# Layer two's row-major causal mask moves from TensorE to VectorE in a two-layer transformer kernel

## What is computed

```
xn = layernorm(x)
x  = x + attention0(xn) + ffn0(xn)              # layer one, 16 heads, gated ffn of width 704
xn = layernorm(x)
# layer two: latent attention, 16 heads of 16 features, latent width 64
c      = layernorm(xh @ Wdkv) * ln_g + ln_b
scores = (xh @ absorbed) @ c.T / sqrt(64)
scores = where(tril, scores, -inf)              # the causal mask
w      = softmax(scores)
x = x + (w @ (c @ Wuv)) @ Wo_h @ Wo.T + bo + experts(xn)   # 32 experts, top 6, and a shared one
```

## Time and profile before

| | us |
|---|---|
| median of three runs | 2020.04 (2015.65 to 2021.65) |
| the profiled execution | 2017.58, its span 2015.8 |
| TensorE busy | 1746.5 |
| VectorE busy | 1100.9 |
| GpSimd busy | 874.7 |
| ScalarE busy | 819.5 |
| VectorE, maxima of `q_rows` (L1224), 256 times | 130.6 |
| TensorE, mask products of `q_rows` (L1611), 256 times | 70.6 |

### The profile page before, as it was taken

The page is one execution under the profiler, slowest core; times in us unless marked ns, Lnnn a source line. Parts: engine busy times, 40 slices in busy tenths (PEclk is TensorE's granted clock), DMA queues, the critical chain, the costliest instruction groups (busy, mean ns, idle before and its releaser), DMA issues.

```text
span 2015.8 us, 41842 instructions
## 1 busy us (share of the span) xinstructions
PE 1746.5 (87%) x16112; PEld 1333.6 (66%) x16112; DVE 1100.9 (55%) x2557; ACT 819.5 (41%) x1596; POOL 874.7 (43%) x995
## 2 busy tenths in 40 slices
PE   3657898989999998989989898999989899888887
PEld 2434676767677676767767676776767677675766
DVE  5645373655647365664737465473746547364442
ACT  2532435344343534334353433435353443534332
POOL 2312343535354454435444353534535353543455
PEclk7878999999999999999999999999999999999999
DMA  5632222313142231314132141413213141321221
GB/s 129 163 85 62 59 59 64 81 43 87 37 102 53 74 73 51 76 40 105 47 83 64 51 87 36 107 37 91 56 53 85 37 107 37 93 54 46 54 64 33
DMA packets 323318, 139.26 MB, mean 69 GB/s; under 512 B 227568, under 2 KB 308528, under 8 KB 323120
## 3 DMA queue, kind: packets, MB, share of 16 engines
q1 hardware_dynamic: 304688, 86.23, 18.5%
q0 software_dynamic: 18432, 50.36, 9.1%
HBM read 102.12 MB, written 29.88 MB: 65 GB/s over the span
## 4 chain that ended last, share of the span: by engine, by line
PE 26%; issue 25%; DVE 19%; POOL 17%; ACT 8%; SPq 3%; DMA 2%; POOLq 0%; DVEq 0%; ACTq 0%
PE s3r L1394 7%; POOL gs L762 6%; POOL h2l L771 5%; POOL cb L741 3%; PE s2acc L1391 3%; DVE th L1269 3%; DVE mx L1102 3%; PE s1a L1394 2%; DVE gs L1274 2%; PE s2r L1394 2%; PE s1acc L1497 2%; POOL h1p L706 2%; PE s1a L1514 2%; ACT h2h L967 1%; ACT p L876 1%
## 5 line engine op out<-in xcount | busy, mean ns | idle before, releaser
L771 POOL TENSOR_TENSOR h2l<-th,h2h 128x512 f16<-128x512 f32 (+1 forms) x224 | 246.5, 1103 | 390.9 <-ACT h2h L967 380.5
L762 POOL TENSOR_TENSOR gs<-gs,cb 128x512 f32<-128x512 f32 x192 | 243.9, 1270 | 263.6 <-DVE gs L1274 262.2
L967 ACT CAST h2h<-th 128x512 f16<-128x512 f32 (+1 forms) x224 | 131.2, 586 | 425.8 <-DVE th L1269 356.9
L1394 PE MATMUL s3r<-xe,xg 128*128 128x256 f16 x2304 | 284.5, 273 | 2.7 <-DVE gs L1274 2.7
L1391 PE MATMUL s2acc<-xd,h2h 128*128 128x256 f16 x1536 | 263.9, 274 | 24.5 <-POOL h2l L771 24.5
L1394 PE MATMUL s3r<-xe,xu 128*128 128x256 f16 x2304 | 283.0, 273 | 1.6 <-DVE th L1269 1.6
L1394 PEld LDWEIGHTS s3r<-xe,xg 128*128 128x128 f16 x2304 | 222.7, 98 | 39.9 <-DVE gs L1274 8.7
L1394 PEld LDWEIGHTS s3r<-xe,xu 128*128 128x128 f16 x2304 | 223.7, 98 | 31.6 <-DVE th L1269 5.5
L741 POOL DMA_DIRECT2D cb<-comb_d x384 | 229.0, 604 | 20.9 <-issue 11.2
L1274 DVE SCALAR_TENSOR_TENSOR gs<-th,s3r 128x512 f32<-128x512 f32 (+1 forms) x224 | 143.9, 642 | 148.8 <-ACT th L971 148.4
L1269 DVE TENSOR_TENSOR th<-s3r,gs 128x512 f32<-128x512 f32 x192 | 132.1, 688 | 168.5 <-POOL gs L762 164.5
(11 more groups left out here) (280 smaller groups left out, 3140.4 us busy)
## 6 DMA issues: line engine op xcount, KB each, us to landing
cb<-comb_d POOLq DMA_DIRECT2D x128, 192.0 KB, 3.4
part_d<-part SPq DMA_DIRECT2D x32, 512.0 KB, 3.3
cb<-comb_d POOLq DMA_DIRECT2D x128, 128.0 KB, 3.0
stacks<-part_d SPq DMA_DIRECT2D x192, 64.0 KB, 2.4
va<-v_d SPq DMA_DIRECT2D x512, 8.0 KB
cb<-comb_d POOLq DMA_DIRECT2D x128, 64.0 KB, 3.0
land<-part_d SPq DMA_DIRECT2D x96, 64.0 KB, 2.7
part<-part_d SPq DMA_DIRECT2D x96, 64.0 KB, 3.5
```

Of the source, the lines that this page charges most:

```text
L762: g.tensor_tensor(gc2[:, p % 2, :], gs2[:, p % 2, :], cb2[:, 2 * (p % 6):2 * (p % 6) + 2, :].rearrange("p a s -> p (a s)"), ALU.mult).then ...
L771: g.tensor_tensor(h2l[0:m, n % 2, 0:w], th2[0:m, n % 2, 0:w], h2h[0:m, n % 2, 0:w], ALU.subtract).then_inc(sem("h2l_made"), 1)
L967: s.copy(h2h[0:m, n % 2, 0:w], th2[0:m, n % 2, 0:w]).then_inc(sem("h2h_made"), 1)
L1394: ins = nc.tensor.matmul(bk, lhs[i][k], rhs[j][k], start=first, stop=last)
```

## The change

The mask products of layer two's row-major scores leave TensorE. `maskq1` becomes 256 columns wide: 128 zeros, then the causal block. VectorE runs, for each head, two instructions that add the mask, write the sum back into the bank in place, and keep the row maximum: one over columns 0 to 127 with the causal block, one over columns 128 to 383 with all of `maskq1`. Each writes its maximum straight into `mx2`, so `m32` and the folding go, and TensorE's transposition waits for the last bank's release. The wait for the bank is put on an instruction of its own (`carry`). All 25 order strings are other ones of the same lengths and the same counts of digits; the body's strings of TensorE and VectorE are shown.

```diff
-        "body": ("022020012122001121002101022221120220212100142212101012131301200103100101031101310120001003"
-                 "34300300403040003043343303001333133"),
+        "body": ("022201021222010100101201202211220200112121021221121201301302001041001010331013110010030203"
+                 "14300300403040003403313030333403133"),
...
-        "body": ("020202011120012120010212122020212212012102021211120121130103001100001000303003010112100002"
-                 "44033040340330331030314303310333431"),
+        "body": ("020212021100210101200212212022120210021110212212121101023210300101001120000000031310130410"
+                 "43033304000004333130300331341330334"),
...
-        maskq1 = sb("maskq1", [P, P], BF16)
+        maskq1 = sb("maskq1", [P, S], BF16)
...
-                v.tensor_reduce(m32[:, h, :], bk[:, 0:3 * P].rearrange("p (c n) -> p c n", n=P), AX.X, ALU.max).then_inc(empties2(u), 1)
-                if n == H - 1:
-                    dve.wait_ge(*emptied2(it, u))
-                    v.tensor_copy(mx2[:, :, 0], m32[:, :, 0]).then_inc(sem("max2_folded"), 1)
-                    v.tensor_tensor(mx2[:, :, 1], m32[:, :, 1], m32[:, :, 2], ALU.max).then_inc(sem("max2_folded"), 1)
+                carry(dve, "dve_waited")
+                v.tensor_tensor_reduce(bk[:, 0:P], bk[:, 0:P], maskq1[:, P:S], 1.0, -3.0e38, ALU.add, ALU.max, mx2[:, h, 0:1])
+                v.tensor_tensor_reduce(bk[:, P:3 * P], bk[:, P:3 * P], maskq1[:, :], 1.0, -3.0e38,
+                                       ALU.add, ALU.max, mx2[:, h, 1:2]).then_inc(empties2(u), 1)
...
-            v.tensor_scalar(maskq1[:, :], mask_tmp[1], -BIG, None, ALU.add).then_inc(sem("dve_const"), 1)
+            v.memset(maskq1[:, 0:P], 0.0)
+            v.tensor_scalar(maskq1[:, P:S], mask_tmp[1], -BIG, None, ALU.add).then_inc(sem("dve_const"), 1)
...
-                    mm(bk[:, P * j:P * j + P * (j + 1)], query(qst2, h, OPEN)[:, P * j:P * j + P],
-                       key(kst2, h, OPEN)[:, 0:P * (j + 1)], start=j == 0, stop=False, skip_group_check=True)
-                mm(bk[:, 0:3 * P].rearrange("p (c n) -> p c n", n=P)[:, 0:3:2, :], identb[:, :],
-                   maskq1[:, :].unsqueeze(1).to_broadcast([P, T, P]), start=False, stop=True,
-                   skip_group_check=True).then_inc(fills2(u), 1)
+                    ins = mm(bk[:, P * j:P * j + P * (j + 1)], query(qst2, h, OPEN)[:, P * j:P * j + P],
+                             key(kst2, h, OPEN)[:, 0:P * (j + 1)], start=j == 0, stop=j == T - 1, skip_group_check=True)
+                ins.then_inc(fills2(u), 1)
                 if n % 2:
                     yield
-            pe.wait_ge(*event("max2_folded", it, 2))
+            pe.wait_ge(*emptied2(it, U2["q_rows", H - 1]))
```

More of the change, by code:

```diff
@@ L81 @@
     "sp": {
[L82 to L91, removed]
+        "body": ("020121001110000112201112102321311101112220301300230331002002203023200132020021031304330323"
+                 "03200021200144411034143001003003110"),
@@ new lines @@
+        "start": ("230011010310112020300201020300120003102211023004121013030231130041142312012020200133030013"
+                 "31020401313101214022013201302403210"),
+        "first": ("111001023131200001012010220313100330020001312011330313022202313102222123011412003100110341"
+                 "32002000040021042100034313100312402"),
+        "late": ("202201000201112022110012221201111110122210103132002332304021031042233243022100033300101303"
+                 "10034000303300141014000101013000331"),
@@ L92 @@
+        "end": ("402041221000010141001201112002213001210010020120013233333320321021233103002303123343011100"
+                 "01000001110113013202222030030101424"),
     },
     "pe": {
-        "body": ("022020012122001121002101022221120220212100142212101012131301200103100101031101310120001003"
-                 "34300300403040003043343303001333133"),
-        "start": ("200201120110120100000311100022002402000120001030001130103323023312204102130041332101330121"
-                 "01243103103221023312234302140103101"),
@@ new lines @@
+        "start": ("100100010000311010020100020000210020013003212210233004311031014111202000224102121230311242"
+                 "13033122300232232303131401301334110"),
+        "first": ("012004102011122133210013001302000303120101002211101203100101201201311101031211302301230024"
+                 "03312004010040000222420303333403322"),
+        "late": ("220201201222002141010221001220224411202021121212101103213102133001301400100130101300131031"
+                 "00030300003030300214000340313310333"),
@@ L104 @@
+        "end": ("200200040210120104221010212212041002000021224221211210020102010100031213103421031110030033"
+                 "01331310033001330101304033130331023"),
     },
     "dve": {
-        "body": ("020202011120012120010212122020212212012102021211120121130103001100001000303003010112100002"
-                 "44033040340330331030314303310333431"),
-        "start": ("000020200002021220310010000000211220110100301312001013030043213001330012214011124022331010"
-                 "11302132341111123200212032301334343"),
@@ new lines @@
+        "start": ("020122102110011200003011000200000000020212030324113033231142312332042312301003010101031011"
+                 "11130230020114010210203432413323201"),
+        "first": ("010011022211102303001121000200031200110212230211130300101010020000101300001311011140112233"
+                 "23410323214034220300020432433323320"),
+        "late": ("022102201421021201200100122024122210012212121112121220101311310300402130140001000100100333"
+                 "00030133000403300033010430131333330"),
@@ L116 @@
+        "end": ("221100012212100002012220112112222022112411142211210000230040102331102010031310310004010000"
+                 "40000033031310003433331033031331003"),
     },
     "act": {
[L118 to L127, removed]
+        "body": ("021222001110221201100022210101222000011201201000210212011223113101201010311310000033241043"
+                 "00020403043030043130300133331343303"),
@@ new lines @@
+        "start": ("111212000221101000021311200000020010011202120010010301230200333040332401301002110322232311"
+                 "11402103333413001040021211332300243"),
+        "first": ("211220112103001011103320120000200201000101123110201002100223113111310131120210123220403003"
+                 "24012300340200402320300403033303341"),
+        "late": ("024041022004022211200101121220222110411121022220121241310130000010031133321010101011300000"
+                 "10303003200014302303000301333333103"),
@@ L128 @@
+        "end": ("220021000102101021000221011220021204012102202020420120122310100311113113211344331101042300"
+                 "33021300334013000330001313033013000"),
     },
     "gp": {
[L130 to L139, removed]
+        "body": ("022001104222100100224022120221202020120021102002002000100300343111330000300012111100123011"
+                 "03413301113331400203313431033011331"),
@@ new lines @@
+        "start": ("123011000131101414231014220200102403303013301100000043233023220100022021131132201432100110"
+                 "01110223202031001220332013110003000"),
+        "first": ("202220200031042030201110124102103020100100304212201010120033031331002201243303313020240100"
+                 "10133001023412300033012110123111101"),
+        "late": ("202412422200042201200112022102101012022212012111200001033010011110040301300201031303030031"
+                 "14003331113310231302031300330040301"),
@@ L140 @@
+        "end": ("221221214041014022202100100222200000011102201120011111020422231303120001110104033033100110"
+                 "13120310330003330331100300333020430"),
     },
@@ L269, in program @@
         mx2 = sb("mx2", [P, H, T])
-        m32 = sb("m32", [P, H, 3])
         mt2 = sb("mt2", [2 * H, P], F16)
```

## The result

The changed kernel takes 2048.6 us (median of four runs, 2041.15 to 2050.32) against 2020.85 for the kernel before: a ratio of 1.0135, interval 1.0117 to 1.0153. It is 28 us slower, where 24 us faster was forecast. The profiled execution has a span of 2046.0 us.

A forecast was written before the change was run, and what follows sets the result against it. TensorE was taken to bound the loop: 15 x 1.76 = 26 us less, +2 for separate waits, takes 2017.6 to 1993.6; 2.4 more for the median gives 1996 us (1985 to 2008; wider range 1979 to 2022).

The forecast's parts named there:

- three signs of being wrong: A 256-element addition over 0.50 us, starts not overlapping, or first query stretch over 5 us away from 172.9.
- four of its cases: Body period: 114.3 us as forecast, 113.4 if better, 116 if the gain doesn't arrive, 117.4 if slower.
- So the loop is TensorE's.: Steady loop: TensorE busy 106.2 of 116.1 us a pass, some 10 us of small gaps, owned by no one engine.
- 15 x 1.76 = 26 us for the mask products: TensorE, 15 passes: 16 mask products a pass at 0.11 us each removed, so 26 us saved.
- The count of the stretch: Layer-two query stretch: TensorE 13.6 us, VectorE 12.4, plus 0.6 for the last pair's turn: 14.2, as now (14.3).
- 24 matmuls x 0.11 = 2.6 us of work have left the rest of the pass.: Outside the query stretch: new strings move matmuls into it, taking 2.6 us of TensorE work from the rest.
- Rival (1): Gain doesn't arrive: redrawn strings leave new gaps of 1.8 us a pass, giving 15 x 1.76 back; 2020 us, chance 0.14.
- A head of 0.55 us: VectorE, query stretch: a head's 128- and 256-element additions take 0.21 + 0.34 us, 0.08 more than now.
- Rival (2): VectorE can't overlap the additions writing PSUM in place: a head 0.88 us, 2039 us in all; chance 0.12.
- Stands at separate waits: +2 us: VectorE's heads: 0.12 us in 35 of 256 cases, 4 us in all, half booked; bounds 0 and 31 us.
- In 'first' and before nothing is booked.: Before the body: TensorE has 90 us of 171 and a clock of 0.75, so no mask saving counted.
- The break-even of rival (2): Query stretch: gain turns to loss where 16h + 3.6 + 0.5 = 16.9, a VectorE head of 0.80 us.

The follow-up runs named there:

- e6: Kernel before with the low parts' product left out of every experts' down (52 matmuls a pass less on TensorE): 1995.2 us, ratio 0.9853 to 0.9909.
- e10: Kernel before with SyncE issuing the twelve loads of layer two's stacks ahead of the routing weights' save: 2012.0 us, ratio 0.9935 to 0.9970.
- e3: Kernel before with the row-major mask product left out and nothing in its place, old strings: 2006.7 us, ratio 0.9906 to 0.9951.
- e5: Changed kernel with the masked sums written to a buffer in SBUF, not back into the PSUM bank: 2042.5 us, ratio 1.0077 to 1.0129.
- e7: e1 with the wait for the bank on the first addition itself, sums in PSUM, old strings: 2030.8 us, ratio to before 1.0034 to 1.0068.
- e9: e5b with the wait for the bank on the first addition itself: 2011.8 us, ratio to before 0.9938 to 0.9973.
- e1: Changed kernel with all 25 order strings of the kernel before, masks still added by VectorE: 2038.2 us, ratio to before 1.0063 to 1.0114.
- e2: Kernel before with all the redrawn order strings, mask products and plain maxima kept: 2061.2 us, ratio 1.0183 to 1.0271.
- e5b: Changed kernel with masked sums written to SBUF and all order strings of the kernel before: 2022.1 us, ratio to before 0.9996 to 1.0025.

## Why the prediction was wrong

A correction first: the experts have 14 units a sequence (the shared expert's 128 and 64 features, and twelve of 256 features), not the 26 of the section on the kernel before. The counts of matmuls in the prediction don't hang on it.

The prediction's count of a body pass was 0.1 us less in the stretch and 2.6 less in the rest; it booked 1.76 of these 2.7. Measured were 1.9 more in the stretch and 0.1 less in the rest. So two things failed: the rest gave nothing back (1 and 4), and the stretch was counted too short (2, 3, 5 and 6). None of the three signs of being wrong that it named showed up (a 256-element addition lasts 0.47 us, starts overlap, the first query product moved by 4.0 us), though the body's period of 118.5 us lay above all four of its cases.

1. *"So the loop is TensorE's."* This step failed for the rest of the pass, and 4 and 8 hang on it. Busy 106 of 116 us and many small gaps were read as an engine at its bound. In its place the runs show a pass that waits, at its first query product, for loads that SyncE issues behind the save of the routing weights, while TensorE's work fits into gaps ahead of it. A gap of 0.35 us for a DMA at the start of the stretch was the visible end of that wait; I treated it as a detail. e6 shows it: 5.5 us of matmuls less a pass, 1.3 us less time, 0.9 of it in the stretch. The new order in SyncE's queue takes 9 us off by itself (e10). What sets the time of that save, some 94 us after the transposition, stays open.

2. *15 x 1.76 = 26 us for the mask products.* Measured by itself 13 us (e3). Nothing speaks against the step of 0.11 us (e6's stretch is 0.9 us shorter for 7 matmuls less); VectorE, at 12.9 of 13.4 us, took back the other half.

3. *The count of the stretch: 13.6 us for TensorE, 12.4 for VectorE, and 0.6 for the last pair, so 14.2.* Measured 15.9 in most passes, 16.2 as mean. VectorE's part was short by 16 x 0.08 = 1.3 us. The sum of two engines' totals also leaves out that two banks couple them: TensorE waits 2.2 us for the maxima and VectorE 2.5 us for products. How the excess splits between the two isn't shown; e5, with heads of 0.55, still has 15.3 us in its quickest passes.

4. *"24 matmuls x 0.11 = 2.6 us of work have left the rest of the pass."* They left, and the time stayed (102.24 against 102.33): TensorE stands 1.0 us longer for the loads and 1.5 us longer in its other gaps. Rival (1) had named this for a loss of the gain and no more. In fact the stretch pays for the moved work and nothing is given back, so the strings alone cost 41 us.

5. *A head of 0.55 us.* Measured 0.63. The lower bound was taken because no row showed a surcharge for PSUM. The fill's row had no reading with it. e5 shows that the write is the surcharge. Rival (2), no overlap and 0.88 (its four durations add up to 0.87), didn't happen: starts overlap in the loop as in the setup, by 0.07 to 0.09 us. The Trainium skill (VectorE: DVE Perf Modes, "The DRAIN you can't avoid") adds to the rule that the prediction took from it that a next instruction which is not held starts earlier, and the prediction left that out. The trace agrees with this exception and not with the rule, and the slower result doesn't confirm the rule.

6. *Stands at separate waits: +2 us.* 7 to 10 us (e7, e9). The price of 0.12 us was near the 0.14 between e1's and e7's shortest distance from product to addition. I counted only stands that the profile lists (35), while most of the cost is in stands too short to be listed (109 heads of e1 start at that distance), and they fall in a stretch that is VectorE's.

7. *"In 'first' and before nothing is booked."* The first query product came 4.0 us later (176.9), and in e2 4.1 us. Part of that may be chance: the four runs with new strings for the setup have 175.4 to 177.3, the ten with the old ones 172.0 to 175.9. The bound of 10 us held.

8. The break-even of rival (2), a head of 0.80 us, was wrong for the same reason as 4: it credits 2.6 us of shed work. Under the old strings, and with the separate wait, the time is level with the kernel before at a head of about 0.56 us (e5b, 1.0010, interval 0.9996 to 1.0025).

## What to carry to other kernels

A busy share of 91% with many small gaps doesn't make an engine the bound: take work away from it off the path and look at the period, or look for the one wait in the pass that ends in a DMA, and follow it back through its queue. Work moved from one stretch of a pass to another costs where it arrives and is only paid back where its engine was the bound (24 matmuls: 2.2 us in the stretch, none from the rest); cut the pass at fixed milestones and compare the parts. When an operation goes to an engine that has a stretch of its own near saturation, its price there has to include where it writes and how it waits.

## What the runs showed of the hardware

- A Vector addition with an accumulated maximum that writes PSUM steps by 0.38 us at 256 elements and its accumulator read lasts 0.14 us; writing SBUF, with the same PSUM input, 0.35 and 0.08.
- The wait on an instruction of its own cost 7.4 (e1 to e7) and 10.3 us (e5b to e9) over 256 heads, 0.03 and 0.04 us a head. Behind it an addition starts 0.18 us or more after the product it waits for, with the wait on the addition itself 0.04 us. It cost nothing where it was met: in the changed kernel the next head's addition starts with the last read (1008.45), in 0.38 us as in e7.
- Twelve loads of 64 KB on SyncE's queue take 5.55 us of issues, 0.46 us each (6.26 us in e10), and that was on the path.
